# Edge stage of a graph kernel: VectorE operations that read one SBUF tensor, and edge gathers that signal in batches of eight

## The chip, the cores and the metric

The kernel runs on one core of a Trainium2 chip. The metric is device time in microseconds (us), the median over runs of the whole kernel. Engines are named as in the profile: PE (TensorE), PEld (its weight loads), DVE (VectorE), ACT (ScalarE), POOL (GpSimd) and SP (SyncE).

## The reference

Two graph layers over N = 50,000 nodes with 128 features and E = 25,000 edges (`src`, `dst`), each followed by a layer norm of `x + layer(x)`:

```
# layer 1, for each edge
f = elu([x[src], x[dst], x[src]-x[dst], attr] @ Wf + bf) * (attr[:,0] < 8)
a = tanh((x[src] @ Wq) * (f @ Wk) * 128**-0.5 @ Wa)
z = exp(a) / exp(segment_sum(a, src))[src] * f
x = layernorm(x + (x + segment_sum(z, src)) @ Wu + bu)
# layer 2: edges both ways, weights normed by their sum at the destination
f(y) = segment_sum(y[src3] * e3, dst3)     # four hops k1..k4, Runge-Kutta
x = layernorm(x + y)
```

Layer 2 needs the 2E directed edges sorted by destination, and for each node the row in which its sum ends.

## The kernel before

**Edge stage.** It runs over NS = 49 supersteps `s` of ST = 512 edges (Q = 4 tiles of 128). POOL issues indirect DMAs: per superstep four gathers `xs` (L340) and four `xd` (L347) from the input, each 128 rows, and four accumulating scatters `agg<-summed` (L330). The gathers of superstep `s` wait until PE has transposed those of `s-3`. From `s = AHEAD = 9` on, POOL also puts away finished supersteps, up to two in each `s`, and later the one of `s-2` after `xd(s)`; a scatter waits for `sc_done` (DVE, L749) and `r_copied` (ACT copy of the sums, L463). PE turns the gathered rows, multiplies (L418 to L421) and adds up edges of one source within the superstep with the 0/1 matrix `same` (L378).

DVE's queue for a superstep, in order: `mask` (L697); `same`, four operations of 128x512 that compare `key_row` (the 512 source numbers, the same on each partition) with each partition's key (L702); a part of a bitonic sort of the 2E edge codes (supersteps 0 to 18, L586 and L587, `flip`); for supersteps 18 to 42 the one-hot matrices `hot_hi` of a histogram over destinations, four operations of 125x392 (L633), whose other factor `sign_lo` ACT makes (L475); then, after the matmuls, `neg` (L720); `earlier`, the number of earlier edges of the same key, four operations over 128, 256, 384 and 512 columns that multiply with the constant triangle `before` and add up (L724); `act_f` (L729, and L735, four of 128x128); the logits (L741); the scatter's rows (L743 to L749); and `za = act_f * exp_att` (L753), which PE's L378 needs. Two lines carry what is changed in form:

```python
v.tensor_tensor(hot_hi[n % HR][:, :, :], pos[...].to_broadcast([EP, HG, HI]),
                hi_f[...].to_broadcast([EP, HG, HI]), ALU.is_equal)
v.scalar_tensor_tensor(junk[:, a, 0:c], key_row[par][:, 0:c], key[...], before[:, a, 0:c],
                       ALU.is_equal, ALU.mult, accum_out=earlier[...])
```

**Node stage.** SP streams node chunks in and out, and ACT, PE and DVE compute layer 1's output. POOL meanwhile gathers the C = 392 columns of sorted edges, `edge_s<-edge_d` (L884), 128 rows of 32 bytes each, one after the other with no wait; they count on two semaphores, one for each half of 196 (`edge_in`). DVE waits for them at the end of the stage (L976).

**Hops and end.** Four hops each gather 392 columns `gx` (L1124) in NB = 49 batches of B = 8, with a wait before each batch; then 391 gathers `ag` of the result (L1341) and the last norm.

Of the kernel before, what the change touches and what calls it, by code (L numbers as in the profile page):

```python
# [5 lines left out]
F32 = mybir.dt.float32  # L6
F16 = mybir.dt.float16
I32 = mybir.dt.int32
ALU = mybir.AluOpType
# [4 lines left out]
D = 128  # L14
# [3 lines left out]
Q = 4  # L18
ST = Q * 128
NS = -(-E // ST)  # L20
NT = NS * Q
# [19 lines left out]
B = 8  # L41
NB = C // B
CH = C // 2
# [4 lines left out]
EP, EC = 125, 200  # L48
# [3 lines left out]
HI = 98  # L52
HG = 4
NHG = 2 * EC // HG
HR = 8

CODES = 25
# [41 lines left out]
def build(nc, x, src, dst, e_in, ea_in, Wf, bf, Wq, Wk, Wa, Wu, bu, out):  # L99
# [9 lines left out]
    with ExitStack() as ctx:  # L109
        def sb(name, shape, dt=F32, stage=None):  # L110
            return (stage or ctx).enter_context(nc.sbuf_tensor(name, shape, dt))

        def sem(name):
            return ctx.enter_context(nc.semaphore(name))
# [6 lines left out]
        pos = sb("pos", [128, ST])  # L121
        part = sb("part", [128, Q])
# [4 lines left out]
        key = sb("key", [128, 2 * NT])  # L127
        node_idx = sb("node_idx", [128, 2 * NT], I32)
        spare = sb("spare", [128, Q])
        before = sb("before", [128, Q, ST])  # L130
        attr = [sb(f"attr{i}", [128, Q, EF + 1]) for i in range(3)]
        za = [sb(f"za{i}", [128, Q, AW]) for i in range(2)]
        junk = sb("junk", [128, Q, ST])
        keyf = sb("keyf", [128, C])
        edge_id = sb("edge_id", [128, C], I32)
# [14 lines left out]
        held = ctx.enter_context(ExitStack())  # L150
# [15 lines left out]
        hi_f = sb("hi_f", [EP, 2 * EC], F32, held)  # L166
        lo_up = sb("lo_up", [EP, 2 * EC], F32, held)
# [14 lines left out]
        earlier = sb("earlier", [128, NT], F32, held)  # L182
        sc_tmp = sb("sc_tmp", [128, NT], F32, held)
# [35 lines left out]
         exp_set, z_ready, r_done, half_copied, r_copied, att_put, n_earlier, sc_set, sc_done) = (  # L219
# [3 lines left out]
                 "n_earlier", "sc_set", "sc_done"))  # L223
# [6 lines left out]
        with nc.Block() as block:  # L230
# [276 lines left out]
            def _(v):  # L507
# [32 lines left out]
                for a in range(Q):  # L540
                    v.tensor_scalar(before[:, a, :], pos[:, :], part[:, a:a + 1], None, ALU.is_lt
                                    ).then_inc(const_set, 1)
                for i in range(2):
                    v.memset(za[i][:, :, :], 0.0).then_inc(za_set, 1)
                v.wait_ge(const_set, 8)
                v.wait_ge(za_set, 2)
# [3 lines left out]
                def codes():  # L550
# [17 lines left out]
                    v.tensor_copy(hi_f[:, :], part_of[:, 0, :]).then_inc(code_set, 1)  # L568
                    v.tensor_scalar(lo_up[:, :], part_of[:, 1, :], -1.0, 0.5, ALU.mult, ALU.add).then_inc(code_set, 1)
                    v.tensor_scalar(ends_i[:, :, :], ends_f[:, :, :], float(BIAS), None, ALU.add).then_inc(code_set, 1)  # L570
                    v.wait_ge(code_set, 24)
# [57 lines left out]
                def high_parts(s):  # L629
                    for n in range((s - HIST0) * GROUPS, (s - HIST0 + 1) * GROUPS):  # L630
                        if n >= HR:
                            v.wait_ge(counted, n - HR + 1)
                        v.tensor_tensor(hot_hi[n % HR][:, :, :],  # L633
                                        pos[0:EP, 0:HI].unsqueeze(1).to_broadcast([EP, HG, HI]),
                                        hi_f[:, n * HG:(n + 1) * HG].unsqueeze(2).to_broadcast([EP, HG, HI]),
                                        ALU.is_equal).then_inc(hi_set, 1)
# [56 lines left out]
                for s in range(NS):  # L693
# [7 lines left out]
                    for a in range(Q):  # L701
                        t = v.tensor_scalar(same[par][:, a, :], key_row[par][:, :], key[:, s * Q + a:s * Q + a + 1],  # L702
                                            None, ALU.is_equal)
# [18 lines left out]
                    for a in range(Q):  # L722
                        c = (a + 1) * 128
                        t = v.scalar_tensor_tensor(junk[:, a, 0:c], key_row[par][:, 0:c], key[:, s * Q + a:s * Q + a + 1],  # L724
                                                   before[:, a, 0:c], ALU.is_equal, ALU.mult,
                                                   accum_out=earlier[:, s * Q + a:s * Q + a + 1])
                    t.then_inc(n_earlier, 1)
                    v.wait_ge(ex_set, s + 1)
# [9 lines left out]
                    v.wait_ge(n_earlier, s + 1)  # L738
                    for j in range(Q):
# [13 lines left out]
                    v.tensor_tensor(za[par][:, :, 0:D], act_f[:, :].rearrange("p (j f) -> p j f", j=Q),  # L753
                                    exp_att[:, :].unsqueeze(2).to_broadcast([128, Q, D]), ALU.mult
                                    ).then_inc(z_ready, 1)
# [103 lines left out]
        edge_in = [sem(f"n_edge_in{i}") for i in range(2)]  # L859
# [21 lines left out]
        def node_gpsimd(g):  # L881

            for c in range(C):
                g.indirect_dma_start(edge_s[:, c, :], None, edge_d[:, :], bass.IndirectOffsetOnAxis(  # L884
                    ap=edge_id[:, c:c + 1], axis=0)).then_inc(edge_in[c // CH], 16)

            for i in range(2):
                g.wait_ge(n_written[i], (NCH + 2 - i) // 2 * 16)
# [48 lines left out]
        def node_vector(v):  # L937
# [36 lines left out]
            for i in range(2):  # L974
                cs = slice(i * CH, (i + 1) * CH)
                v.wait_ge(edge_in[i], CH * 16)  # L976
                v.tensor_tensor(far[:, cs], edge_s[:, cs, 0], keyf[:, cs], ALU.subtract).then_inc(far_set, 1)
                v.wait_ge(far_set, i + 1)
                v.tensor_scalar(far_i[:, cs], far[:, cs], 0.0, None, ALU.max).then_inc(far_i_set, 1)
# [420 lines left out]
```

## Time and profile before

| what | value |
|---|---|
| median of 3 runs | 4009.34 us (4005.22 to 4010.04) |
| profiled execution, its own time | 4005.84 us |
| its span | 4003.9 us |
| busy PE / DVE / ACT / POOL | 865.0 / 2286.9 / 1211.9 / 2966.9 us |
| mean granted TensorE clock | 0.621 |

The span is the time from the first to the last instruction of the profiled execution; what lies around it is 1.9 us. POOL's busy time here is the issuing of indirect DMAs: the instruction is busy while it makes its descriptors, not while the data move.

### The profile page before, as it was taken

Reading aid. Unit: us, or ns where it says so; the run is one execution under the profiler, and the core shown is the slowest. Engines: PE = TensorE matmul, PEld = TensorE weight load, DVE = VectorE, ACT = ScalarE, POOL = GpSimd, SP = SyncE. Lnnn points to the kernel's source line nnn. Section 1 sums busy time; section 2 is a strip of 40 time slices with the busy share of each in tenths; the row PEclk is TensorE's granted clock in tenths of the full one; section 3 lists DMA queues with packets and bytes.
Section 4 is the critical chain, followed back from the end, with each engine's and each line's share of the span. In section 5 each row is a group of like instructions: output and inputs, shape, how many; then the busy total and the mean of one; then the engine's idle time right before and its main releaser. Section 6 shows DMA issues by size and latency. Waiting matters only on the chain.

```text
span 4003.9 us, 25580 instructions
## 1 busy us (share of the span) xinstructions
PE 865.0 (22%) x5636; PEld 736.9 (18%) x5636; DVE 2286.9 (57%) x5661; ACT 1211.9 (30%) x2640; POOL 2966.9 (74%) x2952
## 2 busy tenths in 40 slices
PE   4746777765777000000000000000000000000000
PEld 3745565664555000000000000000000000000000
DVE  6867555553998016555466665666656666633333
ACT  1213666741787001111122221222221222133333
POOL 5778877776777777777677776777767777677776
PEclk8877988987999555555555555555555555555555
DMA  8543333333887013333356665566654444455565
GB/s 270 135 64 63 74 67 62 63 67 72 251 259 236 8 12 106 106 106 106 107 200 211 211 211 188 199 210 210 210 196 141 158 158 158 160 142 156 157 161 139
DMA packets 311964, 581.62 MB, mean 145 GB/s; under 512 B 93856, under 2 KB 172246, under 8 KB 311810
## 3 DMA queue, kind: packets, MB, share of 16 engines
q1 hardware_dynamic: 192034, 394.81, 29.5%
q0 software_dynamic: 116576, 169.55, 19.4%
q10 hardware_dynamic: 3200, 15.63, 1.2%
q8 instruction: 45, 0.74, 0.1%
q14 instruction: 109, 0.89, 0.1%
HBM read 332.00 MB, written 247.75 MB: 145 GB/s over the span
## 4 chain that ended last, share of the span: by engine, by line
POOL 55%; issue 18%; DMA 1%; DVE 1%; ACT 0%; POOLq 0%; PE 0%; DVEq 0%; ACTq 0%
POOL gx L1124 36%; POOL edge_s L884 9%; POOL ag L1341 9%; DVE psum L1229 0%; DMA u<-cross,first_idx 0%; DMA gx<-u,far_row 0%; DVE us L1239 0%; DMA total<-cross_sum,first_idx 0%; DVE psum L1210 0%; DVE tn L1194 0%; DMA u<-us 0%; ACT psum L1175 0%; ACT normed L839 0%; DMA out_dram<-normed 0%; DMA gx<-x,far_i 0%
## 5 line engine op out<-in xcount | busy, mean ns | idle before, releaser
L1124 POOL DMA_INDIRECT gx<-u,far_row x1176 | 1109.7, 944 | 368.7 <-issue 357.5
L1210 DVE TENSOR_TENSOR psum<-gx,psum 128x1024 f32<-128x1024 f32 (+1 forms) x200 | 241.6, 1208 | 711.0 <-DMA gx<-u,far_row 505.0
L1175 ACT ACTIVATE psum<-us 128x512 f32<-128x512 f32 x288 | 173.1, 601 | 1186.0 <-DVE tn L1194 626.3
L884 POOL DMA_INDIRECT edge_s<-edge_d,edge_id x392 | 375.9, 959 | 133.3 <-issue 126.4
L1124 POOL DMA_INDIRECT gx<-x,far_i x392 | 373.4, 952 | 119.5 <-issue 119.5
L1341 POOL DMA_INDIRECT ag<-total,fin_idx x390 | 369.8, 948 | 122.4 <-issue 118.6
L1229 DVE TENSOR_TENSOR_SCAN psum<-goes_on,psum 128x1024 f32<-128x1024 f32 (+1 forms) x200 | 449.1, 2246 | 2.0
L1145 PE MATMUL psum<-last_z,chain 128*128 128x128 f32 x8 | 3.2, 501 | 2002.8 <-DVE last_z L1235 2002.8
L330 POOL DMA_INDIRECT agg<-summed,sc_idx x196 | 325.3, 1660 | 81.7 <-issue 57.2
L1145 PEld LDWEIGHTS psum<-last_z,chain 128*128 128x128 f32 x8 | 2.0, 310 | 2003.7 <-DVE last_z L1235 2003.7
L1163 ACT COPY goes_on<-cont_in 128x1024 f32<-128x1024 f32 (+1 forms) x200 | 202.8, 1015 | 394.7 <-DVE cont_in L1008 201.9
L839 ACT ACTIVATE normed<-res,shift,rstd 128x128 f32<-128x128 f32 (+1 forms) x782 | 313.5, 479 | 0.1
L340 POOL DMA_INDIRECT xs<-in_x_dram,node_idx x196 | 196.4, 1002 | 98.3 <-issue 57.6
L475 ACT ACTIVATE sign_lo<-pos,lo_up 125x512 f16<-125x512 f32 x400 | 252.6, 710 | 0.0
L347 POOL DMA_INDIRECT xd<-in_x_dram,node_idx x196 | 207.3, 1057 | 59.7 <-issue 59.1
L1367 DVE SCALAR_TENSOR_TENSOR res<-xc,ag 128x768 f32<-128x768 f32 x66 | 62.6, 948 | 315.6 <-issue 284.7
L1239 DVE TENSOR_TENSOR us<-psum,inv 128x1024 f32<-128x1024 f32 (+1 forms) x200 | 238.5, 1193 | 0.0
L1194 DVE TENSOR_TENSOR tn<-psum,tp 128x512 f32<-128x512 f32 x288 | 198.1, 688 | 58.9 <-ACT psum L1175 58.9
L720 DVE TENSOR_SCALAR neg<-psum 128x512 f32<-128x512 f32 x49 | 33.8, 690 | 331.7 <-PE psum L421 331.7
L378 PE MATMUL psum<-za,same 128*128 128x132 f32 x1568 | 186.1, 278 | 3.0 <-DVE za L753 3.0
L378 PEld LDWEIGHTS psum<-za,same 128*128 128x128 f32 x1568 | 181.7, 192 | 3.2 <-issue 3.2
L809 DVE BATCH_NORM_STATS2 stats<-res 128x6 f32<-128x128 f32 (+1 forms) x782 | 164.2, 280 | 4.5
(173 smaller groups left out, 2974.8 us busy)
## 6 DMA issues: line engine op xcount, KB each, us to landing
u<-us SPq DMA_DIRECT2D x144, 512.0 KB, 3.1
total<-tn SPq DMA_DIRECT2D x144, 512.0 KB, 3.2
tp<-total SPq DMA_DIRECT2D x98, 512.0 KB, 5.3
ag<-agg SPq DMA_DIRECT2D x65, 396.0 KB
x<-normed SPq DMA_DIRECT2D x65, 387.0 KB, 2.9
xc<-x SPq DMA_DIRECT2D x65, 387.0 KB, 4.6
tp<-u SPq DMA_DIRECT2D x49, 512.0 KB, 5.2
xc<-in_x_dram SPq DMA_DIRECT2D x65, 384.0 KB
```

Of the source, the lines that this page charges most:

```text
L330: g.indirect_dma_start(agg[:, :], bass.IndirectOffsetOnAxis(ap=sc_idx[:, s * Q + j:s * Q + j + 1], axis=0), summed[s % NSUM][:, j, :], Non ...
L347: g.indirect_dma_start(xd[s % 3][:, j, :], None, x[:, :], bass.IndirectOffsetOnAxis(ap=node_idx[:, c:c + 1], axis=0)).then_inc(x_in[s % 3] ...
L378: t = pe.matmul(r_bank[b // 2][:, b % 2 * AW:(b % 2 + 1) * AW], same[s % 2][:, a, b * 128:(b + 1) * 128], za[s % 2][:, a, :], start=(a == ...
L475: act.activation(sign_lo[n % HR][:, i % HG, :], pos[0:EP, :], ACT.Sign, bias=lo_up[:, c:c + 1]).then_inc(lo_set, 1)
L839: t = act.activation(normed[s % 2][0:P, r, 0:D], res[s % 4][0:P, r, :], ACT.Identity, bias=shift[s % 4][0:P, r:r + 1], scale=rstd[s % 4][0 ...
L884: g.indirect_dma_start(edge_s[:, c, :], None, edge_d[:, :], bass.IndirectOffsetOnAxis(ap=edge_id[:, c:c + 1], axis=0)).then_inc(edge_in[c ...
L1124: g.indirect_dma_start(gx[b % 4][:, j * width:(j + 1) * width], None, source[:, :], bass.IndirectOffsetOnAxis(ap=idx[:, c:c + 1], axis=0)) ...
L1163: act.copy(goes_on[i % 2][:, 0:n * D].rearrange("p (f j) -> p f j", j=n), cont_in[:, b * B + c0:b * B + c1].unsqueeze(1).to_broadcast([128 ...
L1210: return v.tensor_tensor(zf.rearrange("p (h f) j -> p j h f", h=H), by_head(gxv(b % 4)[:, c0:c1, 0:D]), per_head(wt[:, b * B + c0:b * B + ...
L1229: v.tensor_tensor_scan(z, goes_on[i % 2][:, 0:(c1 - c0) * D], z, 0.0, ALU.mult, ALU.add).then_inc(run_set, 1)
L1239: return v.tensor_tensor(by_head(us[b % 3][:, c0:c1, :]), zf.rearrange("p (h f) j -> p j h f", h=H), per_head(inv[:, b * B + c0:b * B + c1 ...
L1341: g.indirect_dma_start(ag[s % 4][0:P, r, 0:D], None, total[2][:, :], bass.IndirectOffsetOnAxis(ap=at, axis=0)).then_inc(o_row[s % 4], 16)
```

## The change

In the edge stage `hot_hi` is made by four operations of 125x98 for each one of 125x392, from an f16 copy `pos_h` of the positions and with the edge's number as a scalar. `same` is made in two pieces for tiles 1 to 3: the columns ahead of the tile's own with a sum into `ahead`, the rest as before; `earlier` then runs over the tile's own 128 columns alone, with a `before` of 128x128, and a small addition joins the two. `za` is made by four operations with a scalar each. In the node stage the gathers count on four semaphores by batches of eight, and before each batch POOL waits for the batch two back.

```diff
-        before = sb("before", [128, Q, ST])
+        before = sb("before", [128, 128])
+        pos_h = sb("pos_h", [EP, HI], F16, held)
+        ahead = sb("ahead", [128, NT], F32, held)
-                for a in range(Q):
-                    v.tensor_scalar(before[:, a, :], pos[:, :], part[:, a:a + 1], None, ALU.is_lt
-                                    ).then_inc(const_set, 1)
+                v.tensor_scalar(before[:, :], pos[:, 0:128], part[:, 0:1], None, ALU.is_lt).then_inc(const_set, 1)
+                v.memset(ahead[:, :], 0.0).then_inc(za_set, 1)
+                    v.tensor_copy(pos_h[:, :], pos[0:EP, 0:HI]).then_inc(code_set, 1)
...
-                        v.tensor_tensor(hot_hi[n % HR][:, :, :],
-                                        pos[0:EP, 0:HI].unsqueeze(1).to_broadcast([EP, HG, HI]),
-                                        hi_f[:, n * HG:(n + 1) * HG].unsqueeze(2).to_broadcast([EP, HG, HI]),
-                                        ALU.is_equal).then_inc(hi_set, 1)
+                        for i in range(HG):
+                            t = v.tensor_scalar(hot_hi[n % HR][:, i, :], pos_h[:, :], hi_f[:, n * HG + i:n * HG + i + 1],
+                                                None, ALU.is_equal)
+                        t.then_inc(hi_set, 1)
...
-                        t = v.tensor_scalar(same[par][:, a, :], key_row[par][:, :], key[:, s * Q + a:s * Q + a + 1],
-                                            None, ALU.is_equal)
+                        c = a * 128
+                        k = key[:, s * Q + a:s * Q + a + 1]
+                        if a:
+                            v.tensor_scalar(same[par][:, a, 0:c], key_row[par][:, 0:c], k, 0.0, ALU.is_equal, ALU.add,
+                                            accum_out=ahead[:, s * Q + a:s * Q + a + 1]).then_inc(n_ahead, 1)
+                        t = v.tensor_scalar(same[par][:, a, c:ST], key_row[par][:, c:ST], k, None, ALU.is_equal)
...
-                        c = (a + 1) * 128
-                        t = v.scalar_tensor_tensor(junk[:, a, 0:c], key_row[par][:, 0:c], key[:, s * Q + a:s * Q + a + 1],
-                                                   before[:, a, 0:c], ALU.is_equal, ALU.mult,
+                        c = slice(a * 128, (a + 1) * 128)
+                        t = v.scalar_tensor_tensor(junk[:, a, 0:128], key_row[par][:, c], key[:, s * Q + a:s * Q + a + 1],
+                                                   before[:, :], ALU.is_equal, ALU.mult,
                                                    accum_out=earlier[:, s * Q + a:s * Q + a + 1])
                     t.then_inc(n_earlier, 1)
+                    v.wait_ge(n_earlier, s + 1)
+                    v.wait_ge(n_ahead, (s + 1) * (Q - 1))
+                    v.tensor_tensor(earlier[:, tile], earlier[:, tile], ahead[:, tile], ALU.add).then_inc(n_earlier2, 1)
...
-                    v.tensor_tensor(za[par][:, :, 0:D], act_f[:, :].rearrange("p (j f) -> p j f", j=Q),
-                                    exp_att[:, :].unsqueeze(2).to_broadcast([128, Q, D]), ALU.mult
-                                    ).then_inc(z_ready, 1)
+                    for j in range(Q):
+                        t = v.tensor_scalar(za[par][:, j, 0:D], act_f[:, j * 128:(j + 1) * 128], exp_att[:, j:j + 1],
+                                            None, ALU.mult)
+                    t.then_inc(z_ready, 1)
...
-        edge_in = [sem(f"n_edge_in{i}") for i in range(2)]
+        edge_in = [sem(f"n_edge_in{i}") for i in range(4)]
...
             for c in range(C):
+                k = c // B
+                if c % B == 0 and k >= 2:
+                    g.wait_ge(edge_in[(k - 2) % 4], ((k - 2) // 4 + 1) * B * 16)
                 g.indirect_dma_start(edge_s[:, c, :], None, edge_d[:, :], bass.IndirectOffsetOnAxis(
-                    ap=edge_id[:, c:c + 1], axis=0)).then_inc(edge_in[c // CH], 16)
+                    ap=edge_id[:, c:c + 1], axis=0)).then_inc(edge_in[k % 4], 16)
...
-                v.wait_ge(edge_in[i], CH * 16)
+                last = ((i + 1) * CH - 1) // B
+                for n in range(4):
+                    v.wait_ge(edge_in[n], ((last - n) // 4 + 1) * B * 16)
```

## Rows read from the trace of the kernel before

**Rows 1.** The page: span, and the chain that ended last (shares of the span).
```profile
span 4003.9 us, 25580 instructions
...
POOL 55%; issue 18%; DMA 1%; DVE 1%; ACT 0%; POOLq 0%; PE 0%; DVEq 0%; ACTq 0%
```

**Rows 2.** Edge stage's window: PE, PEld, DVE, ACT, POOL busy; PEclk, DMA, GB/s.
```profile
0.00:970.00 970.00, 624.57 (x4191) 555.68 (x4191) 586.47 (x2046) 403.08 (x793) 729.67 (x597) 0.84 0.44 92
```

**Rows 3.** Waits of POOL, whole span: us in total, times, longest.
```profile
POOL gx L1124 <- issue: 477.0, 1565, 0.3
POOL edge_s L884 <- issue: 126.4, 391, 4.7
...
POOL xs L340 <- PE psum L409: 30.4, 5, 12.4
...
POOL agg L330 <- DVE sc_idx L749: 8.3, 6, 3.8
```

**Rows 4.** Windows of POOL alone: supersteps 19 to 43, 44 to 47, node stage.
```profile
377.05:853.02 475.97, 377.90 (x301) 0.88 0.36 66
853.02:925.58 72.56, 57.94 (x48) 0.81 0.38 70
...
990.00:1120.00 130.00, 98.91 (x103) 1.00 0.77 240
```

**Rows 5.** Durations of POOL's scatters and gathers, 395 to 861 us: min/median/max ns.
```profile
L330 POOL DMA_INDIRECT agg<-summed,sc_idx x97: 1553/1573/2981, 393.7 to 851.2; - x97
...
L347 POOL DMA_INDIRECT xd<-in_x_dram,node_idx x99: 940/945/2304, 400.8 to 860.6; - x99
```

**Rows 6.** Timeline of DVE and POOL, 400 to 408 us: start, us.
```profile
400.30 0.88 DVE L735 TENSOR_SCALAR act_f<-act_f,mask 128x128 f32<-128x128 f32 x4
400.81 0.99 POOL L347 DMA_INDIRECT xd<-in_x_dram,node_idx  x1 [0.31 <-issue]
...
403.36 0.70 DVE L753 TENSOR_TENSOR za<-act_f,exp_att 128x512 f32<-128x512 f32 x1
403.99 0.29 DVE L697 TENSOR_SCALAR mask<-attr 128x4 f32<-128x4 f32 x1
404.06 1.67 DVE L702 TENSOR_SCALAR same<-key_row,key 128x512 f32<-128x512 int32 x4
404.59 1.26 POOL L347 DMA_INDIRECT xd<-in_x_dram,node_idx  x1 [0.30 <-issue]
405.65 1.99 DVE L633 TENSOR_TENSOR hot_hi<-pos,hi_f 125x392 f16<-125x392 f32 x4
406.16 2.98 POOL L330 DMA_INDIRECT agg<-summed,sc_idx  x1 [0.31 <-issue]
```

**Rows 7.** Timeline of DVE in the last superstep.
```profile
949.68 0.34 DVE L724 SCALAR_TENSOR_TENSOR junk<-key_row,key,before 128x128 f32<-128x128 int32 x1
...
949.95 0.48 DVE L724 SCALAR_TENSOR_TENSOR junk<-key_row,key,before 128x256 f32<-128x256 int32 x1
...
950.89 0.75 DVE L724 SCALAR_TENSOR_TENSOR junk<-key_row,key,before 128x512 f32<-128x512 int32 x1
...
951.56 0.69 DVE L729 SCALAR_TENSOR_TENSOR act_f<-psum,ex 128x512 f32<-128x512 f32 x1
```

**Rows 8.** Timelines of ACT and POOL around one scatter.
```profile
635.01 0.38 ACT L463 COPY summed<-psum 128x264 f32<-128x264 f32 x1
...
636.45 1.92 POOL L330 DMA_INDIRECT agg<-summed,sc_idx  x1 [0.30 <-issue]
```

**Rows 9.** Timeline of POOL in the node stage; landing of the hops' gathers.
```profile
1126.36 0.94 POOL L884 DMA_INDIRECT edge_s<-edge_d,edge_id  x1 [4.71 <-issue]
...
1376.81 0.95 POOL L884 DMA_INDIRECT edge_s<-edge_d,edge_id  x1 [3.13 <-issue]
...
DMA to landing us min/median/max: 2.4/2.6/6.1
```

**Rows 10.** DVE's waits for PE in supersteps 19 to 43 (groups by line).
```profile
L720 DVE TENSOR_SCALAR neg<-psum 128x512 f32<-128x512 f32 x25 | 17.3, 691 | 192.8 <-PE psum L421 192.8
```

More of the change, by code:

```diff
@@ L55 @@
 HR = 8
-CODES = 25
+CODES = 26
 R = 6
@@ L218, in build @@
         (turned, turned_sb, mm_done, same_set, mask_set, neg_set, ex_set, act_set, logit_set, att_set,
-         exp_set, z_ready, r_done, half_copied, r_copied, att_put, n_earlier, sc_set, sc_done) = (
+         exp_set, z_ready, r_done, half_copied, r_copied, att_put, n_earlier, n_ahead, n_earlier2,
+         sc_set, sc_done) = (
              sem("a_" + n) for n in (
@@ L222, in build @@
                  "logit_set", "att_set", "exp_set", "z_ready", "r_done", "half_copied", "r_copied", "att_put",
-                 "n_earlier", "sc_set", "sc_done"))
+                 "n_earlier", "n_ahead", "n_earlier2", "sc_set", "sc_done"))
         t_src, t_dst, t_attr, b_h, b_t = bank[0], bank[1], bank[2], bank[3], bank[4]
@@ L539, in _ @@
                 v.tensor_scalar(first_row[:, :], pos[:, 0:128], 0.0, None, ALU.is_ge).then_inc(const_set, 1)
-                for a in range(Q):
-                    v.tensor_scalar(before[:, a, :], pos[:, :], part[:, a:a + 1], None, ALU.is_lt
-                                    ).then_inc(const_set, 1)
+                v.tensor_scalar(before[:, :], pos[:, 0:128], part[:, 0:1], None, ALU.is_lt).then_inc(const_set, 1)
                 for i in range(2):
                     v.memset(za[i][:, :, :], 0.0).then_inc(za_set, 1)
-                v.wait_ge(const_set, 8)
-                v.wait_ge(za_set, 2)
+                v.memset(ahead[:, :], 0.0).then_inc(za_set, 1)
+                v.wait_ge(const_set, 5)
+                v.wait_ge(za_set, 3)
                 v.tensor_scalar(first_row[:, :], first_row[:, :], ident[:, 0:1], None, ALU.mult).then_inc(const_set, 1)
@@ L568, in codes @@
                     v.tensor_copy(hi_f[:, :], part_of[:, 0, :]).then_inc(code_set, 1)
+                    v.tensor_copy(pos_h[:, :], pos[0:EP, 0:HI]).then_inc(code_set, 1)
                     v.tensor_scalar(lo_up[:, :], part_of[:, 1, :], -1.0, 0.5, ALU.mult, ALU.add).then_inc(code_set, 1)
                     v.tensor_scalar(ends_i[:, :, :], ends_f[:, :, :], float(BIAS), None, ALU.add).then_inc(code_set, 1)
-                    v.wait_ge(code_set, 24)
+                    v.wait_ge(code_set, 25)
                     v.tensor_scalar(ends_i[:, :, :], ends_i[:, :, :], SHIFT, None, ALU.logical_shift_left
@@ L737, in _ @@
                     v.wait_ge(act_set, s * (Q + 1) + Q + 1)
-                    v.wait_ge(n_earlier, s + 1)
+                    v.wait_ge(n_earlier2, s + 1)
                     for j in range(Q):
```

## Prediction

> **What bounds the kernel now.** I read the chain that ended last first: POOL and its issue gaps are 73% of the span of 4003.9 us, every other engine at most 1% [rows 1]. So the kernel is one long queue of indirect DMAs. The window of the edge stage confirms it: POOL is busy 729.67 of 970 us, and between two issues lie about 0.30 us more [rows 2, 3]. Next the waits of POOL: nearly all are "issue" gaps of 0.3 us, which the change leaves alone; 30.4 us are waits for PE in five early supersteps, 8.3 us for DVE's scatter rows [rows 3]. DVE can therefore change the time in three ways only: by slowing the issues themselves, by making POOL wait in the early supersteps, or through the chain that leads to `r_copied`.
>
> Does DVE slow the issues? The shortest gather takes 940 ns and the shortest scatter 1553, the longest 2304 and 2981 [rows 5]. The timeline shows when: a scatter that starts 0.5 us after four back-to-back `hot_hi` operations takes 2.98 us, and its surplus of 1.43 us is what was left of the group; a gather beside `same` takes 1.26; one beside the four L735 operations 0.99 [rows 6]. Operations with two SBUF tensors, back to back, hold POOL up to the end of their group; single-source ones for 0.05 to 0.32 us.
>
> **hot_hi.** A superstep of eight gathers and four scatters costs at least 8 x 0.940 + 4 x 1.553 = 13.73 us busy. In supersteps 19 to 43 it is 377.90 / 25 = 15.12, in 44 to 47, with the same DVE work but `hot_hi`, 57.94 / 4 = 14.49 [rows 4]. So `hot_hi` costs POOL 0.63 us a superstep, 15.8 us in all (25 supersteps). What replaces it are 16 single-source operations, the nearest row being L735: 0.88 us for four of 128 columns, so 0.22 each and 3.5 us for sixteen against 1.99 for four of the old. Their price on POOL is not shown. From below it is nothing. At L735 it is 0.05 us for a group of four, 0.2 a superstep. From above it is the rate of `same`, 0.32 us on 1.67, which on 3.5 us is 0.67 a superstep and takes the whole gain. I take the 0.2, since size and form are L735's: -15.8 + 5 = -10.8 us. DVE's own 1.5 us more are hidden: it waits 192.8 / 25 = 7.7 us a superstep for PE before `neg` [rows 10].
>
> The Trainium skill (SBUF — State Buffer, on the shared port pair) says that a DVE operation in a 2-port mode, or one with two SBUF inputs against a GpSimd operation that reads SBUF, holds the pair exclusively for its whole instruction. That speaks against this change, since it makes the single-source operations lockers too. By that rule the price would go with the length held, 0.63 x 3.5 / 1.99 = 1.11 us a superstep, a term of +12 us in place of -10.8; the row of `same` (0.32 us against 1.43) agrees that they hold POOL up, but for less.
>
> **same, earlier, za.** `earlier` moves on by 0.27 us at 128 columns and 0.67 at 512, 1.88 for the four [rows 7]; four at 128 cost 1.08, so -0.80. `same` goes from 1.67 to seven pieces. The plain ones, between 0.22 at 128 and 0.42 at 512, make 0.42 + 0.35 + 0.29 + 0.22 = 1.28. The three with a sum are not in the trace: at the pace of `earlier` 0.27 + 0.40 + 0.54 = 1.21, at the plain pace 0.86. That is +0.82 or +0.47. `za` goes from 0.63 (L753 to L697) to 0.88 [rows 6], +0.25, and the joining addition costs about 0.2, as a small operation like L697 takes. DVE's sum is +0.1 to +0.5 us a superstep. Where it counts, the early supersteps before POOL's five waits, DVE has no gap: 5 x 0.1 to 0.5 is 0.5 to 2.5 us. Against it stand three 512-column operations less for `before` ahead of the first superstep (some 1.4 us) and two small ones more (0.5). I take +1, bounds 0 and +2. On POOL's side `earlier` has two SBUF inputs and shrinks from 1.88 to 1.08 us. Supersteps 44 to 47 have 14.49 - 13.73 = 0.76 us of surplus each from `same`, `earlier` and `za` together. Taking a third of it for `earlier`, and halving that, gives 0.1 us, x 49 = -5; the longer `same` gives back some. I take -2, bounds -5 and +3.
>
> **What is late next.** A scatter needs `r_copied`. In the row it was ready at 635.39 and POOL came for it at 636.14, 0.75 us later [rows 8]. A faster POOL meets this chain (last `xd` landed, PE, ACT, PE, `neg`, `exp`, copy), which the change hardly touches. POOL already waited six times there, 8.3 us in all (the row names the scatter rows, made one operation before; the copy is the other semaphore of that wait) [rows 3]. If half of the 25 supersteps are so tight and lose 0.3 us each, that is +4; if all lose 0.5, +12. I take +3, bounds 0 and +12.
>
> **The gathers.** The waits add 47 instructions. POOL comes to each 8 x 1.25 = 10 us after the last gather it asks for was issued; the hops' gathers land 2.6 us after issue and 6.1 at most [rows 9], and the node stage's DMA share of 0.77 [rows 4] would have to make that 10 to cost anything. Behind the waiting instruction stand all later POOL work and so the end. A satisfied wait costs nothing measurable: `gx`, with one before each batch, has gaps of 0.3 us at most over 1565 [rows 3]. Against this, two gathers of the node stage stand behind gaps of 4.71 and 3.13 us with nothing named, 196 gathers apart [rows 9]. No queue with regular waits has such a gap. That the run of 392 unwaited DMAs causes them is my guess, not shown; if the waits remove them, -(4.41 + 2.83) = -7.2 us; if not, 0. I take -7.
>
> **Sum.** -10.8 - 2 + 1 + 3 - 7.2 = -16 us. The profiled execution's own time is 4005.84, so 3990; the median stands 3.5 us above that execution, so 3993 against 4009.
>
> **Rivals.**
> 1. Only the gathers' gaps stay. For it: no row says what makes them. 3993 + 7 = 4000.
> 2. The new operations hold POOL as long as they save. For it: the rate of `same`, and the skill's rule in the sentence above. Against: L735. The first term becomes +1, and the `r_copied` term falls away: -2 + 1 + 1 - 7 = -7, so 4002; with the whole length of the rule, by its 12 us, 4013.
> 3. The gain is made and eaten: POOL waits for `r_copied` instead. For it: the 0.75 us of rows 8. Against: only the faster supersteps are hit. The +3 becomes +8 to +12: 3998 to 4002.
> 4. Slower: POOL gets in only when a whole group ends, as behind the old `hot_hi`. Then chance and length of the delay both grow with the group: 0.63 x (3.5 / 1.99)^2 = 1.95 us, +1.3 a superstep, +33 us in place of -10.8; without the `r_copied` term the sum is +25 us, 4034. It decides from about 1.0 us a superstep on (break-even of the sum). Against it: `same` is four such operations back to back and lets POOL in after 0.32 us.
>
> **How the numbers follow.** A measurement of this kernel can tell about 0.2%, 8 us, from no change: below 4001 is faster, above 4017 slower. Forecast 0.40, own range 3984 to 4001. Rival 1 0.20, half of it below 4001. Rival 2 0.20, of which 0.08 below 4001, 0.10 the same and 0.02 slower. Rival 3 0.10, half below. Rival 4 0.10, nearly all slower. Together faster 0.61, same 0.28, slower 0.11. The range leaves out most of rival 4 and the far ends of the bounds (-28 is all of them together): 3983 to 4014.
>
> **What would show it.** Right: supersteps 19 to 43 at about 18.3 us in place of 19.0, no issue above 1.3 us beside `hot_hi`, a POOL surplus near 0.9 us a superstep, no gap of microseconds in the node stage. Wrong: scatters and gathers longer than 2 us beside the sixteen; a larger wait of POOL for the ACT copy; waits on `edge_in` that come late; more than 31 us of waits for PE in the early supersteps.

## The result, and the profile after

The changed kernel takes 3966.44 us (median of 5 runs, 3963.89 to 3969.97) against 4009.34 us in the same session (5 runs, 4005.22 to 4010.79). The ratio is 0.9897 [0.9886, 0.9908]: faster by 43 us. The forecast was 3993 in a range of 3983 to 4014, so the sign was right and the size was not: the time lies 17 us below the range. The profiled execution's own time is 3963.89 us against 4005.84, 41.95 us less.

The page of the kernel after, its span and the chain that ended last:

```profile
span 3962.0 us, 26422 instructions
...
POOL 55%; issue 18%; DMA 1%; DVE 1%; ACT 0%; POOLq 0%; PE 0%; DVEq 0%; ACTq 0%
```

The shares of the chain are those of [rows 1]. Nothing took POOL's place as the bound; its queue got shorter. Four views say where. First the window of the edge stage, to where the first `edge_s` gather is near (columns as in [rows 2]):

```profile
0.00:935.00 935.00, 630.40 (x4191) 562.14 (x4191) 618.49 (x2835) 403.38 (x793) 694.07 (x597) 0.85 0.44 96
```

The same 597 POOL instructions are busy 694.07 us in place of 729.67: 35.6 us less, while DVE is busy 32 us more, which does not lengthen the stage. Then the windows of POOL alone, for supersteps 19 to 43 and 44 to 47, against [rows 4]:

```profile
373.93:821.30 447.37, 351.00 (x301) 0.89 0.37 70
821.30:892.77 71.47, 56.84 (x48) 0.78 0.38 71
```

The 25 supersteps with `hot_hi` take 447.4 us in place of 476.0. Their busy time fell by 26.9 us, nearly the whole of it. What is saved is the issues' own length, as the durations of scatters and gathers show (minimum, median, maximum in ns), against [rows 5]:

```profile
L333 POOL DMA_INDIRECT agg<-summed,sc_idx x96: 1553/1576/1742, 402.0 to 819.4; - x96
...
L350 POOL DMA_INDIRECT xd<-in_x_dram,node_idx x99: 940/944/1142, 396.9 to 829.0; - x99
```

Minima and medians stand where they stood. The longest scatter went from 2981 to 1742 ns and the longest gather from 2304 to 1142. Last the waits of POOL, against [rows 3]:

```profile
POOL edge_s L898 <- issue: 119.2, 391, 0.3
...
POOL xs L343 <- PE psum L412: 34.8, 6, 12.4
```

The gaps of 4.71 and 3.13 us are gone (126.4 to 119.2 us). The early waits for PE grew by 4.4 us.

I call surplus what an issue takes over the shortest of its kind (0.94 us for a gather, 1.553 for a scatter), and say that an issue is beside `hot_hi` when it overlaps that run of operations. Both come from the timelines of POOL and DVE. In supersteps 19 to 43 the surplus went from 34.3 to 7.4 us; what is left of their length after it is nearly the same, 441.7 and 440.0 us. So where the kernel before takes some 4009 us, the length of these supersteps is nearly a constant plus the surplus, and the experiments below are read by it.

### The profile page after: what moved, and what is told of

Read it like the earlier page. It is cut to its first block, busy times and chain, and to the rows that moved or that the text cites. A ratio compares the mean times of both kernels' runs of the same rounds, so it can differ in the third digit from the quotient of the medians.

```text
span 3962.0 us, 26422 instructions
## 1 busy us (share of the span) xinstructions
PE 879.3 (22%) x5636; PEld 748.5 (19%) x5636; DVE 2318.4 (59%) x6450; ACT 1213.3 (31%) x2640; POOL 2931.1 (74%) x2952
## 4 chain that ended last, share of the span: by engine, by line
POOL 55%; issue 18%; DMA 1%; DVE 1%; ACT 0%; POOLq 0%; PE 0%; DVEq 0%; ACTq 0%
POOL gx L1140 37%; POOL edge_s L898 10%; POOL ag L1357 9%; DVE psum L1245 0%; DMA u<-cross,first_idx 0%; DMA gx<-u,far_row 0%; DVE us L1255 0%; DMA total<-cross_sum,first_idx 0%; DVE psum L1226 0%; DVE tn L1210 0%; DMA u<-us 0%; ACT psum L1191 0%; ACT normed L850 0%; DMA out_dram<-normed 0%; DVE psum L1237 0%
## 5 line engine op out<-in xcount | busy, mean ns | idle before, releaser
L898 POOL DMA_INDIRECT edge_s<-edge_d,edge_id x392 | 376.4, 960 | 126.0 <-issue 119.2
L333 POOL DMA_INDIRECT agg<-summed,sc_idx x196 | 313.3, 1598 | 78.4 <-issue 63.8
L350 POOL DMA_INDIRECT xd<-in_x_dram,node_idx x196 | 189.0, 964 | 59.7 <-issue 59.4
L727 DVE TENSOR_SCALAR neg<-psum 128x512 f32<-128x512 f32 x49 | 33.8, 690 | 249.0 <-PE psum L424 249.0
```

Of the source, the lines that this page charges most:

```text
L333: g.indirect_dma_start(agg[:, :], bass.IndirectOffsetOnAxis(ap=sc_idx[:, s * Q + j:s * Q + j + 1], axis=0), summed[s % NSUM][:, j, :], Non ...
```

## The experiments

The runs fell on several chips, and on some of them the kernel before took 4602 to 4636 us. Each ratio is against the kernel before on the same chip, and the text says which chips they were, since on the slower ones POOL also waits in nearly every superstep. The changed kernel itself was timed only where the kernel before takes 4009 us. The letters of the theories are each expectation's own.

**One part at a time, where the kernel before took 4636 us.** Each kernel is the kernel before with one part of the change: hot_hi, `same` with `earlier` and the join, `za`, or the gathers with their semaphores and waits.

> Only hot_hi in single-source pieces. Theory A (formed on the trace after: operations with two SBUF inputs, back to back, cost POOL everything that supersteps 19 to 43 gained beyond the others' 0.3 to 0.4 us each): POOL's surplus over 13.73 us in those supersteps falls from 1.38 to about 0.7 us, the time by 14 to 20 us, to 3989 to 3995. Theory B (the prediction's account): a fall of 11 us, surplus about 0.95. Theory C (a single-source group holds POOL as well): no change.

> Only same and earlier changed. Theory A (earlier with its long two-input operations and same with its long single-source ones cost POOL about 0.4 us a superstep in all 49): 12 to 18 us faster, surplus in supersteps 19 to 43 from 1.38 to about 1.0. Theory B (the prediction): 1 to 2 us faster at most, after what DVE's longer queue costs in the early supersteps.

> Only za in four pieces. Both theories: within 2 us of before; if za's one two-input operation costs POOL as much as a quarter of the hot_hi group, 4 us faster.

> Only the gathers in batches with waits. The gaps of 4.7 and 3.1 us go, 7 us faster (4002); if they come from something else they stay and the time is that of before.

Measured: x1_hot 4618.09 us, 0.9956 [0.9940, 0.9973]; x2_same 4633.49, 0.9994 [0.9984, 1.0005]; x3_za 4632.44, 0.9992 [0.9982, 1.0001]; x4_gathers 4633.38, 0.9994 [0.9985, 1.0004]. These ratios don't carry over to where the kernel before takes 4009 us, and x4_gathers, whose edge stage is that of before, shows why. Its POOL has issued the last `edge_s` gather long before the node stage is done, and waits for it 287.1 us before the first hop; where the kernel before takes 4009 us it doesn't wait there (0.31 us, an issue gap):

```profile
POOL gx L1129 <- DMA x<-normed: 287.1, 1, 287.1
```

So microseconds saved in the edge stage need not shorten the kernel there. And POOL's issues fall otherwise; DVE, then POOL:

```profile
399.71 0.69 DVE L753 TENSOR_TENSOR za<-act_f,exp_att 128x512 f32<-128x512 f32 x1
400.39 1.73 DVE L702 TENSOR_SCALAR same<-key_row,key 128x512 f32<-128x512 int32 x4
402.04 1.98 DVE L633 TENSOR_TENSOR hot_hi<-pos,hi_f 125x392 f16<-125x392 f32 x4
```
```profile
399.90 2.00 POOL L330 DMA_INDIRECT agg<-summed,sc_idx  x1 [3.38 <-issue]
402.21 1.84 POOL L330 DMA_INDIRECT agg<-summed,sc_idx  x1 [0.30 <-issue]
```

Before the first scatter POOL stands still for 3.38 us, and such a stop comes back about every 21.3 us. So nearly each superstep (23 of 25) finds the engines in the same position, with a scatter 0.17 us into `hot_hi` that takes 1.84 us. The surplus beside `hot_hi` is 7.1 us here, with no issue held for more than 1.2 us. In the profiled run of before it was 20.7 us, and 8 issues were held for more than 1.2 us, 11.0 us in all (in x10_idle_waits below, with the same edge stage again, 15.4 us and 5 issues). The DVE program is the same. This was the first sign that the position decides. x3_za shows the same from the other side. Beside `same` only its surplus is 1.9 us, in x4_gathers 11.0; but its scatters now start 1.44 us into `hot_hi` and cost 0.42 us there, so beside `hot_hi` it has 16.1 us, x4_gathers 7.1, and in all 27.3 against 27.0.

**The second input (kernel before at 4007 us).** x6_hot_two_inputs makes `hot_hi` in 16 pieces, but each still reads two tensors:

```
for i in range(HG):
    t = v.tensor_tensor(hot_hi[n % HR][:, i, :], pos[0:EP, 0:HI],
                        hi_f[:, n * HG + i:n * HG + i + 1].to_broadcast([EP, HI]), ALU.is_equal)
```

> The kernel before with hot_hi in 16 pieces that still read two SBUF tensors. If what counts is the second SBUF input, POOL's surplus stays at 1.4 us a superstep or grows, since the pieces take longer in all (no gain, or up to 10 us slower). If what counts is the length of one operation, it falls as with the single-source pieces, to 0.9 or less, and the time by 10 us or more.

Measured: 4034.33 us, 1.0064 [1.0047, 1.0081]. DVE and POOL at the start of one run:

```profile
390.71 2.82 DVE L634 TENSOR_TENSOR hot_hi<-pos,hi_f 125x98 f16<-125x98 f32 x16
```
```profile
391.23 3.80 POOL L330 DMA_INDIRECT agg<-summed,sc_idx  x1 [0.30 <-issue]
```

A scatter that starts 0.52 us into sixteen short operations of 0.18 us each is held for 2.25 us, until the whole run has ended. 16 issues are held for over 1.2 us, the surplus beside `hot_hi` is 42.6 us, and the supersteps take 502.4 us; the kernel is 27 us slower, where the expectation had 10 at most. Shorter operations are thus no help: every issue that starts 0.5 us or more into this run waits for its end. But the start counts too. Nine scatters that start 0.16 to 0.23 us into it cost 0.03 to 0.06 us. And with the old run of four, a start at 0.50 or 0.51 us is always held (8 times before, 5 in x10, once in e19), while one at 0.17 us costs 0.28 or 0.29 us and one at 0.56 or 0.57 us 0.34 or 0.35 (six in x12).

**`same` and its neighbours (at 4007 us).** x7_same_old_earlier makes `same` in the seven new pieces and leaves `earlier` as it was. x9_same_summed gives all four full-width operations of `same` a sum, which makes each longer. x12_all_but_hot is the changed kernel with the old `hot_hi`.

> The kernel before with same in its new seven pieces and earlier as it was; the sums in ahead are made and not used. If same's long single-source operations are what costs POOL, the surplus falls by 0.25 us or more a superstep; if earlier's two inputs are, it stays within 0.1.

> The kernel before with a sum output on each whole row of same (the sums are not used), which should make the operation run at one result a cycle (about 0.75 us in place of 0.50) and not in a mode that uses both ports. If the two-port mode is what costs POOL, the surplus falls by 0.25 us a superstep although DVE works 1 us longer. If the length counts, it grows.

> The changed kernel with the old hot_hi. On a chip whose compute chain is not the bound (supersteps near 19 us), theory A: 42 us gain less hot_hi's 16 to 20, so about 0.6% faster than before, surplus in supersteps 19 to 43 about 1.0 us. Theory B (the prediction: hot_hi 11, the rest of the edge stage 2, the gathers 7): 0.2% faster, surplus 1.3.

Measured: x7 3994.98 us, 0.9965 [0.9952, 0.9977]; x9 3997.89, 0.9979 [0.9970, 0.9989]; x12 3971.17, 0.9910 [0.9893, 0.9926]. The old `hot_hi` is untouched in all three, yet the surplus beside it fell from 20.7 to 6.3, 7.5 and 7.6 us, and no issue is held for over 1.2 us. A longer `same` (x9) brings these issues down as far as a split one. Nearly the whole gain of the change is there without touching `hot_hi` (x12, which also has the new gathers; both theories of its expectation had less).

x9 also shows what `same` itself costs. In the kernel before, eight gathers start 0.53 us into `same` and have a surplus of 0.31 or 0.32 us, as the one of [rows 6]. In x9 eight gathers start at the same point, and have 0.00 or 0.01; in x7, where the operation at that point makes a sum too, ten have as little. DVE and POOL in x9:

```profile
425.34 0.73 DVE L705 TENSOR_SCALAR_CACHE_REDUCE same<-key_row,key 128x512 f32<-128x512 int32 x1
```
```profile
425.87 0.94 POOL L349 DMA_INDIRECT xd<-in_x_dram,node_idx  x1 [0.30 <-issue]
```

So the plain single-source comparison delays an issue and the one with a sum doesn't, though it takes longer.

**The parts again, and one left out (at 4010 us).** e13 and e14 repeat x2 and x1; x15_all_but_same is the changed kernel with `same` and `earlier` as before.

> Only `same`, `earlier` and their join changed, hot_hi, za and the gathers old; the edit of x2_same, here where the kernel before takes about 4006 us. Theory A (POOL's issues wait for the end of a run of VectorE operations that read two tensors only where they start inside it; which issues start inside hot_hi depends on what VectorE does just before, so changing `same` alone already keeps them out): supersteps 19-43 at 18.3 to 18.6 us in place of 19.04, VectorE's shorter `earlier` another few us, both gaps of 5 and 3 us in the old edges' gathers stay, ratio 0.993 to 0.996, so 3978 to 3990 us. Theory B (the prediction's account: hot_hi alone carries the gain, `same` and `earlier` are worth -1): 4004 to 4007 us, ratio 0.999 to 1.000.

> Only hot_hi as in the changed kernel; the edit of x1_hot, here where the kernel before takes about 4006 us. Theory A (the held issues are those inside two-input runs, either edit removes them, so the parts don't add): alone it brings nearly what same and earlier bring alone, 20 to 28 us, supersteps 19-43 at 18.2 to 18.5 us, ratio 0.993 to 0.995. Theory B (each part has its own price, hot_hi's the -11 of the prediction): ratio 0.997, 3996 us. Theory C (everything is additive and x12_all_but_hot leaves hot_hi only 5 us): ratio 0.9985 to 0.999.

> The changed kernel with `same` and `earlier` as they were before (no join): hot_hi and za by the new form, the gathers with their waits. Theory A (parts don't add: hot_hi's edit already frees POOL in the run beside hot_hi): the loss against the changed kernel is 5 to 12 us, 3972 to 3978 us, ratio 0.991 to 0.993. Theory C (additive, same and earlier carry about 28 us): 3992 to 3995 us, ratio 0.9965. Theory B: as the changed kernel within 2 us, 3965 to 3968 us.

Measured: e13 3989.56 us, 0.9951 [0.9931, 0.9970]; e14 3993.44, 0.9958 [0.9943, 0.9973]; x15 3983.38, 0.9935 [0.9913, 0.9956]. Supersteps 19 to 43, in us (surplus split by what the issue overlaps):

| kernel | length | surplus | beside hot_hi | beside same only | elsewhere | held > 1.2 us |
|---|---|---|---|---|---|---|
| before | 476.0 | 34.3 | 20.7 | 5.6 | 8.0 | 8 |
| e14, hot_hi alone | 460.7 | 21.1 | 6.4 | 5.2 | 9.5 | 0 |
| e13, same and earlier alone | 453.8 | 16.0 | 6.2 | 4.9 | 4.9 | 0 |
| x7, same alone | 460.9 | 20.0 | 6.3 | 4.8 | 9.0 | 0 |
| x9, same with sums | 459.8 | 22.3 | 7.5 | 5.1 | 9.7 | 0 |
| x10 (below), as before | 475.0 | 31.0 | 15.4 | 7.1 | 8.5 | 5 |
| x15, all but same and earlier | 456.8 | 16.2 | 4.5 | 1.6 | 10.2 | 0 |
| x12, all but hot_hi | 453.7 | 13.7 | 7.6 | 1.4 | 4.7 | 0 |
| after | 447.4 | 7.4 | 2.0 | 1.4 | 4.0 | 0 |
| x6, hot_hi in 16, two inputs | 502.4 | 57.2 | 42.6 | 5.9 | 8.7 | 16 |

Read down the columns. `hot_hi` alone saves 15.3 us of length and `same` with `earlier` alone 22.2, but both with `za` only 28.6: each by itself leaves no issue held, 8 before and 5 in x10, on the chip of e13 and e14. (What e14 keeps beside `hot_hi` are issues of 0.2 to 0.3 us of surplus that began beside `same`.) The last column but one falls from 8 to 10 us to 4 to 5 wherever `earlier` is new, and the one beside `same` only falls to 1.4 to 1.6 where `za` is new: the operation ahead of `same` in DVE's queue is `za`, with two inputs before, and an issue that starts beside it (at 0.19 us into it, 0.44 us of surplus for a scatter) reaches into `same`. This gives `earlier` and `za` about 4 us each. `za` by itself was timed only at 4636 us, so its share is read from this table and not from a run of its own; by x3_za, with the old `hot_hi` behind it, it can come to nothing.

In whole times the parts come nearer to adding up. `hot_hi` is worth 0.42% alone (e14) and 0.13% as the last part (x12 to the changed kernel), `same` with `earlier` 0.49% alone (e13) and 0.38% as the last (x15), with intervals of 0.1 to 0.2% on each ratio. e14 and x15 lie between the ranges of their theories A and their additive rivals, so that the parts don't add rests on the table, from one trace of each kernel.

The cleanest line is in e14. DVE, then POOL:

```profile
466.40 1.67 DVE L704 TENSOR_SCALAR same<-key_row,key 128x512 f32<-128x512 int32 x4
467.99 2.85 DVE L636 TENSOR_SCALAR hot_hi<-pos_h,hi_f 125x98 f16<-125x98 f16 x16
```
```profile
466.94 1.25 POOL L348 DMA_INDIRECT xd<-in_x_dram,node_idx  x1 [0.30 <-issue]
468.49 0.94 POOL L348 DMA_INDIRECT xd<-in_x_dram,node_idx  x1 [0.30 <-issue]
```

Here as in [rows 6] a gather falls beside the old `same` and takes 0.31 us too long, and with the gap of 0.30 us the next issue starts 0.50 us into `hot_hi`. In the kernel before all 8 issues in that position, each right behind such a delayed gather, were held to the end of the run (six gathers of 2.30 us, two scatters of 2.98). In x6 the gathers there took 3.12 to 3.13 us. Beside the single-source operations it takes 0.94 us, the shortest a gather can be. So the chain of causes reads: `same`, by delaying one issue, puts the next one where `hot_hi` holds it. Change either and the 11 us are gone (e14; x7 and x9, where the delay is gone, but where `hot_hi` also starts later, and which of the two frees the next issue isn't told apart). In e13 the corresponding issue starts 0.48 us into the old run and has a surplus of 0.07 us; there the run lasts 2.03 us in place of 1.98, as if VectorE had waited this time. Why those 0.02 us are enough isn't shown, only that they are.

**Alignment, by itself.** x16 puts one more operation of 0.46 us between `same` and `hot_hi` in the 25 supersteps; x17 puts it ahead of `same`:

```
if HIST0 <= s < HIST0 + HISTN:      # x16: behind the loop that makes same; x17: ahead of it
    v.tensor_scalar(pad[:, 0:256], key_row[par][:, 0:256], key[:, s * Q:s * Q + 1], 0.0,
                    ALU.is_equal, ALU.add, accum_out=pad[:, 256:257])
```

> The kernel before with one more VectorE operation of some 0.47 us (256 columns of key_row compared and summed, one result a cycle, its output used by nothing) in each of the 25 supersteps with hot_hi, between `same` and hot_hi. Theory C (alignment: GpSimd's issues are let in at ends of `same`'s operations, so the next one starts 0.50 us into hot_hi's run and is held to its end, 8 times with over 1.2 us each; half a microsecond between the two runs moves that start to the run's edge): at most 2 such issues, the surplus of issues beside hot_hi down from 20.7 to 8 to 13 us, supersteps 19-43 at 18.5 to 18.8 us, whole kernel 3990 to 4000 us, ratio 0.996 to 0.998. Theory D (how much is held goes by how long VectorE is in such operations, wherever they stand): surplus unchanged or more, 8 such issues or more, ratio 1.000 to 1.002.

> The control: the same added operation, put ahead of `same`, so that `same` and hot_hi stand to each other as in the kernel before. Theory C: about 8 issues held over 1.2 us as before, surplus beside hot_hi 17 to 23 us, ratio 0.999 to 1.001. Theory D: the same as x16_space_behind_same. If both kernels are faster by the same amount, the alignment with `same` is not what decides.

> The edit of x16_space_behind_same. Where the kernel before takes some 4006 us: theory C (alignment): at most 2 issues beside hot_hi held over 1.2 us (before 8), surplus there 8 to 13 us (before 20.7), supersteps 19-43 at 18.5 to 18.8 us, ratio 0.996 to 0.998. Theory D (time spent in such operations, wherever they stand): 8 such issues, surplus 19 to 22 us, ratio 1.000 to 1.002. Where it takes some 4636 us, this tells no more than x16 did: ratio 0.999 to 1.000.

> The edit of x17_space_ahead_of_same, the control. Where the kernel before takes some 4006 us: theory C: 5 to 9 issues held over 1.2 us, surplus beside hot_hi 16 to 22 us, ratio 0.999 to 1.001. Theory D: as e18_space_behind_again. A ratio below 0.998 with 5 or more issues still held would speak against both: something else than held issues would then set the time.

e18 and e19 repeat x16 and x17. The pairs ran where the kernel before takes 4636 and 4602 us, and so without the 8 held issues that they were made for. Measured: x16 4632.46 us, 0.9995 [0.9986, 1.0005]; x17 4618.99, 0.9965 [0.9953, 0.9977]; e18 4601.27, 0.9994 [0.9983, 1.0005]; e19 4609.54, 1.0014 [1.0002, 1.0025]. x17 and e19 are one kernel, and their whole times disagree in sign, so nothing is concluded from them. The surplus beside `hot_hi` agrees: 6.1 and 6.2 us with the space behind `same`, 13.2 and 16.9 with the same work ahead of it. e18, then e19, DVE and POOL around one run:

```profile
427.16 0.46 DVE L707 TENSOR_SCALAR_CACHE_REDUCE pad<-key_row,key 128x256 f32<-128x256 int32 x1
427.56 1.99 DVE L634 TENSOR_TENSOR hot_hi<-pos,hi_f 125x392 f16<-125x392 f32 x4
```
```profile
427.33 1.59 POOL L331 DMA_INDIRECT agg<-summed,sc_idx  x1 [0.30 <-issue]
429.22 1.76 POOL L331 DMA_INDIRECT agg<-summed,sc_idx  x1 [0.30 <-issue]
```
```profile
608.28 1.99 DVE L634 TENSOR_TENSOR hot_hi<-pos,hi_f 125x392 f16<-125x392 f32 x4
```
```profile
607.67 1.75 POOL L331 DMA_INDIRECT agg<-summed,sc_idx  x1 [0.30 <-issue]
609.73 1.97 POOL L331 DMA_INDIRECT agg<-summed,sc_idx  x1 [0.31 <-issue]
```

The scatters start 0.23 us before and 1.66 into the run in e18, 0.61 before and 1.45 into it in e19, and cost 0.04 + 0.21 against 0.20 + 0.42 us. Equal work in another place costs two to three times as much beside `hot_hi` (over all issues of these supersteps the surplus is 26.4 against 29.2 us and 25.6 against 33.8), so the theory that only the time spent in such operations counts is out. That a shift alone would remove the 8 held issues at 4009 us is left open.

**The gaps in the edges' gathers.** x10_idle_waits puts a wait that is long satisfied ahead of every eighth gather of the kernel before. x11_eight_sems adds no wait, and spreads the signals over eight semaphores:

```diff
+                if c % B == 0:
+                    g.wait_ge(row_set, 1)                 # x10; then as before
...
-                    ap=edge_id[:, c:c + 1], axis=0)).then_inc(edge_in[c // CH], 16)
+                    ap=edge_id[:, c:c + 1], axis=0)).then_inc(edge_in[c // 49], 16)     # x11
```

> The kernel before, with one wait on a semaphore that is long satisfied put ahead of every eighth of the 392 gathers of the sorted edges' data; their signals and semaphores are as before. Theory A (GpSimd's queue stalls only after some 196 issues of an indirect DMA in a row in which it waited for nothing, and any wait resets that): both gaps of 4.7 and 3.1 us are gone, ratio 0.998, 3999 us. Theory B (the gap comes where transfers not yet signalled pile up, and the wait for the batch two back is what prevents it): both gaps stay, ratio 1.000. Theory C (it hangs on the count of one semaphore, 196 transfers to each, which is also how many issues lie between the two gaps): both gaps stay, at the same two issues.

> The kernel before, with the 392 gathers of the sorted edges' data signalling eight semaphores, 49 transfers each, in place of two with 196 each; no wait is added in GpSimd's queue. Theory B (transfers that nobody has waited for pile up, and a wait for earlier ones prevents the stall): both gaps, 4.7 and 3.1 us, at issues 112 and 308, stay; ratio 1.000. Theory C (the count on one semaphore): the gaps go or move; if gone, ratio 0.998.

Measured: x10 4008.86 us, 1.0000 [0.9989, 1.0010]; x11 4637.95 (before 4636.19), 1.0006 [0.9997, 1.0015]. The waits of POOL for `edge_s`, in x10 and in x11:

```profile
POOL edge_s L886 <- issue: 127.8, 391, 6.1
```
```profile
POOL edge_s L884 <- issue: 121.9, 391, 0.9
```

In x10 the gaps stay, of 6.09 and 3.16 us, ahead of the 114th and the 310th gather, where they are in every kernel with the old semaphores, on all these chips. In x11 both are gone without a wait. (The 0.9 is one of a few gaps of 0.86 us that all kernels on the slower chips have.) On x11's own chip x16 and x17, with the old semaphores, have both. Each gap comes when 113 gathers have been issued on one semaphore; with 104 on each at most (x4, x12, x15, after) or 49 (x11) there is none. So it is the number of gathers counted on a semaphore, not the missing wait. The time of x11 didn't fall with them, since on that chip POOL waits 290.8 us for the node stage behind these gathers. Whether it is the issues, their landings or the value that counts wasn't told apart. What it is worth is seen in the length from the first to the last `edge_s` issue: 501.4 us before, 503.0 in x10, 494.7 after.

**Scatters sooner.** y_ahead7 is the changed kernel with AHEAD = 7 in place of 9.

> The changed kernel with the scatters starting two supersteps sooner (from superstep 7, not 9). Its GpSimd waits 34.8 us for TensorE to turn the gathered rows in supersteps 5 to 9, with no scatter to issue meanwhile. If these scatters fill that wait: 8 scatters of 1.55 us less later, 8 to 13 us, 3953 to 3959 us, ratio 0.987. Rival: VectorE bounds these supersteps, the first scatters then wait for the zeroing of agg or for r_copied, and the time stays within 3 us of the changed kernel's.

Measured: 4642.66 us (before 4636.19), 1.0014 [1.0005, 1.0023]. What the rival in the expectation named is there: the first nine supersteps take 177 us, against 125 in the changed kernel where it was timed, and POOL's first scatter waits for the zeroing of `agg`:

```profile
POOL agg L333 <- DMA agg<-zero: 26.8, 1, 26.8
```

Whether AHEAD = 7 gains or loses against the changed kernel isn't shown, since that one has no time on this chip. But y_ahead7 holds the whole change and is 6 us slower than the kernel before, so the gain of 1% isn't shown for such chips either. Where the kernel before takes 4007 to 4010 us, no other version came below the changed kernel's ratio; x12 is nearest.

## Why the prediction was right in sign and wrong in size

**The bound and the three ways** held. POOL's queue sets the time, DVE acts on it through the length of the issues, and the surplus fell by 35.5 us (55.6 to 20.1 over the whole edge stage), the gathers' length by 6.7. From the first instruction to the first `edge_s` issue the kernel is 34.9 us shorter. That the sums meet so well is partly luck: in supersteps 0 to 8, where POOL waits for PE, 2.8 us less surplus brought nothing, and the last superstep is 2.0 us shorter without any.

**hot_hi, forecast -10.8.** The surplus beside it fell by 18.7 us (20.7 to 2.0), and by 14.3 with this edit alone (e14). Both halves of the term were mis-sized. The old price of 0.63 us a superstep was the difference of two means, supersteps 19 to 43 less 44 to 47, and took for granted that the other operations cost the same 0.76 us in both; in 19 to 43 they cost (5.6 + 8.0) / 25 = 0.54, and the run 0.83. The new pieces were put at 0.2 us a superstep, and all issues beside them now have 0.08. The kind of the form, L735's and not that of `same`, was chosen rightly. That two-input operations hold POOL to the end of their group was read from one row; the same trace has eight scatters that start 0.17 us into the run and cost 0.28 or 0.29 us.

**same, earlier, za, forecast -2 with bounds -5 and +3.** This is the step that failed, with -16.8 us: 8.2 in supersteps 19 to 43 (13.6 to 5.4 us outside `hot_hi`) and 8.6 in the other 24 (21.3 to 12.7), of which the 2.8 in supersteps 0 to 8 shortened nothing. `same` with `earlier` alone took 20.7 us off the whole time (e13). I priced `earlier` at half of a third of the surplus and gave `za` and `same` nothing or a loss. The table has about 4 us each for `earlier` and `za` in the 25 supersteps. Supersteps 9 to 18, with up to eight scatters each, went from 240.9 to 236.8 us, by about the 4.4 us of surplus that they lost: nearly as much as the whole bound of -5 for 49 supersteps.

**The edits were summed as if they were independent**, and they aren't. By the table either of the two first edits leaves no held issue; the sum forecast none of that for `same`. In [rows 6] both members of the pair stand one below the other, the gather of 1.26 us beside `same` and the scatter of 2.98 us that starts 1.57 us later; the prediction read them as two prices and not as cause and effect.

**Early supersteps, forecast +1.** Supersteps 0 to 8 take 125.2 us against 123.9, which agrees, but x10 has 133.2 with the same program there, so one trace says little. **r_copied, forecast +3.** Not there: the length less surplus went from 441.7 to 440.0 us. POOL's gaps above 0.3 us in these supersteps add up to 5.0 us, before to 6.7. DVE still waits 127.7 us for PE before `neg`, 192.8 in [rows 10], so its longer queue didn't become the bound. Rival 3 is out.

```profile
L727 DVE TENSOR_SCALAR neg<-psum 128x512 f32<-128x512 f32 x25 | 17.3, 692 | 127.7 <-PE psum L424 127.7
```

**The gathers, forecast -7.2.** Measured -6.7, the right size. The cause that I had guessed, a run without waits, was wrong: x10 waits and keeps the gaps, x11 doesn't and loses them. Rival 1 is out.

**Rivals 2 and 4.** Beside the sixteen single-source operations an issue has at most 0.11 us of surplus (e14) or 0.13 (the changed kernel) where none of it falls on `same`. So they hold POOL for next to nothing. Rival 4 named the right mechanism for the wrong form: x6 has it, with sixteen two-input pieces, 26.4 us more length in the 25 supersteps. The rule of the Trainium skill (SBUF — State Buffer, on the shared port pair) speaks of a lock for a whole instruction. For operations with two SBUF inputs the measurement is harder than the rule, since POOL is held over the ends of a dozen instructions (2.25 us in x6). For the single-source ones, which the rule counts as lockers in their 2-port mode, the delays of 0.2 to 0.3 us beside the plain `same` (0.50 us each) and of 0.13 at most beside pieces of 0.16 us stay below the length of one operation, as the rule has it; it was the prediction that made the price go with the whole group. One gather speaks against that: in x15 it starts 0.14 us into `same`, has 0.71 us of surplus and ends only when the four operations are over.

**What would show it.** No issue stands out beside `hot_hi`; the supersteps take 17.9 us in place of the 18.3 foretold, and the surplus is 0.30 us in each, not 0.9. The early waits for PE are 34.8 us, above the 31 named as a sign of failure, and the kernel is faster all the same: six waits at the start don't judge such a change. The shares given in the prediction add up to 0.63 for faster, 0.25 for the same and 0.12 for slower, each 0.01 to 0.03 off its totals.

## What to carry to other kernels

Where one engine's queue of DMA issues is the bound, list the issues that are longer than the shortest of their kind, with what the other engine does at that moment, and look one issue back: a delay of 0.3 us there can put the next one where it is held for 1.4 us. Prices of single edits taken from such a list need not add up, so time them in pairs or leave one out, and on the chip where the whole is timed. Prefer VectorE operations with one SBUF tensor and a scalar, even when they are more and longer in all, and spread the signals of long runs of indirect DMAs over several semaphores.

## What the runs showed of the hardware that was not expected

Sixteen back-to-back VectorE operations of 0.18 us with two SBUF tensors held a GpSimd issue that started some 0.5 us into them for 2.25 us, and one that started at 0.17 us for 0.03; sixteen with one tensor and a scalar, 0.16 us each, for 0.00 to 0.13 us. A comparison with a sum (x9) held none of the gathers beside it, the plain one delayed them by up to 0.3 us, and once, in x15, by 0.71. An issue of an indirect DMA stalled for 3.1 to 6.9 us after 113 of them on one semaphore, in every kernel that counted 196 on it. A VectorE comparison with a sum takes 0.33, 0.47, 0.60 and 0.74 us for 128, 256, 384 and 512 columns, without one 0.50 us for 512. The same program took 4007 us on one chip and 4636 on another; on the slower one POOL issues the `edge_s` gathers while the node stage nearly stands still, 24 GB/s in the window below of x4_gathers against 168 after, at 1000 to 1400 us, and then waits for that stage, which is why the gaps cost nothing there. What makes the difference stays open. It isn't fixed to the chip: where the kernel before took 4010 us, one of its 19 executions took 4605.

```profile
1100.00:1500.00 400.00, 39.81 (x154) 31.90 (x154) 31.70 (x147) 26.35 (x84) 304.42 (x300) 0.55 0.13 24
```
```profile
1000.00:1400.00 400.00, 204.44 (x1207) 152.93 (x1205) 242.84 (x1166) 215.11 (x680) 303.55 (x317) 0.81 0.54 168
```
